# Reordering a fused two-attention and expert layer: projections moved into the first gap, transposed scores two slots sooner

## Time and profile before

| | |
|---|---|
| median of 3 runs | 625.67 us |
| profiled execution | 623.53 us |
| its span, first to last instruction | 621.8 us |
| PE busy | 521.4 us, 84% of the span |
| DVE, ACT, POOL busy | 55%, 35%, 24% |
| mean granted clock of PE | 0.946 |

### The profile page before, as it was taken

One profiled execution on the slowest core, in us unless ns is written; L12 is line 12 of the kernel. 1 busy time (PEld: TensorE's weight loads), 2 busy tenths in 40 slices (PEclk: granted clock), 3 DMA queues, 4 the chain that ended last, 5 costly groups with the idle time before them and its releaser, 6 DMA issues. The chain is left out here.

```text
span 621.8 us, 12823 instructions
## 1 busy us (share of the span) xinstructions
PE 521.4 (84%) x5092; PEld 404.6 (65%) x5092; DVE 339.1 (55%) x952; ACT 219.7 (35%) x491; POOL 147.3 (24%) x160
## 2 busy tenths in 40 slices
PE   6179395979799989989999789798798999999960
PEld 5047274756567767766767556577587888888850
DVE  2577265456667768768677957674263202232114
ACT  2014143335344544545554535353521111232103
POOL 4000011003004004004104166001124755132330
PEclk9599699889999999999999989799999999999995
DMA  5999907585785595685549556346666634897214
GB/s 163 118 132 139 161 10 127 68 108 69 94 127 82 89 144 70 100 135 69 91 77 136 85 104 191 66 148 190 229 229 228 204 51 74 247 304 241 23 20 138
DMA packets 58119, 78.96 MB, mean 127 GB/s; under 512 B 8734, under 2 KB 51357, under 8 KB 54988
## 3 DMA queue, kind: packets, MB, share of 16 engines
q1 hardware_dynamic: 41192, 39.34, 41.8%
q10 hardware_dynamic: 10724, 33.51, 16.4%
q0 software_dynamic: 6144, 5.29, 5.3%
HBM read 40.32 MB, written 13.74 MB: 87 GB/s over the span
## 5 line engine op out<-in xcount | busy, mean ns | idle before, releaser
L957 DVE TENSOR_REDUCE negm<-nat 128x4 f32<-128x512 f32 (+2 forms) x192 | 120.0, 641 | 84.3 <-PE nat L534 81.1
L769 ACT ACTIVATE probs<-byk 128x512 f32<-128x512 f32 (+1 forms) x192 | 105.6, 563 | 114.9 <-PE byk L534 100.4
L534 PE MATMUL nat<-arena 96*128 96x128 bf16 (+2 forms) x512 | 72.8, 245 | 0.0
L534 PE MATMUL byk<-arena 99*128 99x128 bf16 (+2 forms) x512 | 72.2, 244 | 0.0
L534 PEld LDWEIGHTS byk<-arena 99*128 99x128 bf16 x512 | 46.1, 100 | 17.9 <-issue 1.3
L534 PEld LDWEIGHTS nat<-arena 96*128 96x128 bf16 x512 | 46.6, 101 | 16.4 <-issue 2.5
L530 PE MATMUL nat<-window_q,identb 128*128 128x384 bf16 (+1 forms) x96 | 35.0, 365 | 18.8 <-DMA arena<-parts_k 12.7
L1213 POOL TENSOR_TENSOR resk<-fk,parts_k 128x512 f32<-128x512 f32 x8 | 9.3, 1159 | 158.0 <-ACT fk L710 107.2
L530 PE MATMUL byk<-window_k,identb 128*128 128x384 bf16 (+1 forms) x96 | 34.3, 357 | 13.4 <-DMA arena<-mT 12.7
L672 PE MATMUL work<-yn_T,arena 128*128 128x160 f32 x256 | 40.1, 305 | 2.4 <-DVE r_s L1124 2.4
L672 PE MATMUL work<-woT,arena 128*128 128x160 f32 x256 | 39.8, 304 | 0.0
(11 more groups left out here) (189 smaller groups left out, 912.6 us busy)
## 6 DMA issues: line engine op xcount, KB each, us to landing
arena<-parts_q SPq DMA_DIRECT2D x96, 128.0 KB, 5.1
arena<-parts_k SPq DMA_DIRECT2D x96, 128.0 KB, 5.2
arena<-in_ffn_wi ACTq DMA_DIRECT2D x12, 1024.0 KB, 5.2
arena<-in_ffn_wo ACTq DMA_DIRECT2D x12, 1024.0 KB, 8.3
expert_x<-ranked ACTq DMA_DIRECT2D x4, 650.0 KB, 5.2
v_s<-expert_x SPq DMA_DIRECT2D x20, 130.0 KB
xres<-in_x ACTq DMA_DIRECT2D x8, 256.0 KB, 5.9
token_y<-xres SPq DMA_DIRECT2D x8, 256.0 KB, 4.9
```

Of the source, the lines that this page charges most:

```text
L534: last = nc.tensor.matmul(bank[:, i * w:(i + 1) * w], lhsT, rhs, start=False, stop=(i == heads - 1), skip_group_check=True)
L769: nc.scalar.activation(dst, src, ACT.Exp, scale=0.25).then_inc(exp_ready, 1)
L957: V.tensor_reduce(dst, src, AX, ALU.max, negate=True).then_inc(nat_free[job % 2], 1)
```

## The change

It moves pieces of the plan and one of the loads; no computation is added or left out.

- Unit 2's QS, SQ and KS stand before the first N job, and its SK behind unit 0's first N job. Unit 3's four steps stand where unit 2's stood. `x3`, the input that unit 3's projection reads, is loaded at the start, and the clearing of `v_c` (`one_c`) goes to slot 13.5.
- `SOONER` is 2 for units 2 to 13: their T, PV, YA and YB stand two slots sooner (unit 2's already did).
- MT of units 3 to 13, and XL with it, stand 0.8 slots sooner (13.2 behind n0 and not 14).
- Y2, WO, R3 and L3 stand one slot later behind YB than before, so one slot sooner in all for units 3 to 11 and one later for units 0 to 2. The closing steps of units 4 to 13 that are c units stand two slots sooner, XR and RT about one.

```diff
--- before.py
+++ after.py
@@ -54,12 +54,14 @@
 X_SLOT = (0, 1, 2, 3, 0, 1, 2, 0)
 X_TURN = (1, 1, 1, 1, 2, 2, 2, 3)
 X_BEFORE = {4: 0, 5: 1, 6: 2, 7: 4}
-LOADS = ((-20, "x1"), (-19.9, "x2"), (-19.8, "wv"), (-19.7, "rows"), (-3, "one_s"), (-2, "one_c"), (11.52, "x3"), (11.58, "wo"),
+LOADS = ((-20, "x1"), (-19.9, "x2"), (-19.8, "wv"), (-19.75, "x3"), (-19.7, "rows"), (-1.2, "one_s"), (11.52, "wo"), (13.5, "one_c"),
          (24.7, "ck"), (24.75, "c0"), (24.8, "cq"), (38.3, "c1"), (38.4, "cv"), (50.1, "wr"))
 CLEARS = (4, 5, 6, 7)
 
 
-SOONER = {0: 5.1, 1: 3.4, 2: 2}
+SOONER = {0: 5.1, 1: 3.4}
+SOONER.update({k: 2 for k in range(2, 14)})
+AHEAD = {2: ((-25.5, "QS"), (-25.45, "SQ"), (-25.4, "KS"), (-23.4, "SK")), 3: ((-24.9, "QS"), (-24.45, "SQ"), (-24.4, "KS"), (-24.3, "SK"))}
 ROWS_BY_ACT = 12
 
 
@@ -104,10 +106,10 @@
                             add(n0 + (15.6 if b == 0 else 9.6), "LX", UNIT_OF["s", later])
             if b == 3:
                 add(n0 + 9.7, "LC", UNIT_OF["c", 2])
-            add(n0 + {0: 11.56, 1: 12.65, 2: 13.25}.get(b, 14.05), "XL", k)
-            for at, name in ((-12.9, "QS"), (-12.45, "SQ"), (-12.4, "KS"), (-12.3, "SK")) if b == 2 else ((-19, "QS"), (-18, "SQ"), (-17.5, "KS"), (-16.5, "SK")):
+            add(n0 + {0: 11.56, 1: 12.65}.get(b, 13.25), "XL", k)
+            for at, name in AHEAD.get(b, ((-19, "QS"), (-18, "SQ"), (-17.5, "KS"), (-16.5, "SK"))):
                 add(n0 + at, name, k)
-            for at, name in ((13.95 if b == 0 else 8.5, "VS"), (20, "XB"), (34 - sooner, "Y2"), (35 - sooner, "WO"), (36 - sooner, "R3"), (36.8 - sooner, "L3")):
+            for at, name in ((13.95 if b == 0 else 8.5, "VS"), (20, "XB"), (35 - sooner, "Y2"), (36 - sooner, "WO"), (37 - sooner, "R3"), (37.8 - sooner, "L3")):
                 add(n0 + at, name, k)
         else:
             if b + TOK < B:
@@ -115,14 +117,14 @@
             late = 2 if b == B - 1 else 0
             for at, name in ((-19, "KC"), (-18, "CK"), (late - 11.5, "XC"), (late - 10.2, "QC"), (late - 9.2, "SC"), (late - 6, "XA"), (10, "VC")):
                 add(n0 + at, name, k)
-            for at, name in CLOSING.get(k, ((n0 + 33.3, "FQ"), (n0 + 34.4, "R1"), (n0 + 35.2, "L1"), (n0 + 37, "R2"), (n0 + 37.7, "L2"),
-                                            (n0 + 39.4, "XS"), (n0 + 39.5, "XR"), (n0 + 40.9, "RT"))):
+            for at, name in CLOSING.get(k, ((n0 + 33.3 - sooner, "FQ"), (n0 + 34.4 - sooner, "R1"), (n0 + 35.2 - sooner, "L1"), (n0 + 37 - sooner, "R2"),
+                                            (n0 + 37.7 - sooner, "L2"), (n0 + 39.4 - sooner, "XS"), (n0 + 40.4 - sooner, "XR"), (n0 + 41.8 - sooner, "RT"))):
                 add(at, name, k)
         for j in range(JOBS):
             add(n0 + j, "N", k, j)
             add(t_slot(k, j), "T", k, j)
         add(n0 + (11.3 if k == 0 else 12), "MP", k)
-        add(n0 + {0: 11.5, 1: 12.6, 2: 13.2}.get(k, 14) if k < last else 195.6, "MT", k)
+        add(n0 + {0: 11.5, 1: 12.6, 14: 14}.get(k, 13.2) if k < last else 195.6, "MT", k)
         for g in range(G):
             add(n0 + 22.2 - sooner + 3 * g if k < last - 1 else t_slot(k, 3 * g + 2) + (1.1 if g < G - 1 else 0.5), "PV", k, g)
         add(n0 + 32.6 - sooner if k < last - 1 else (198.6, 206.9)[k - last + 1], "YA", k)
```

## The result

The changed kernel takes 636.84 us in the median of 4 runs (634.86 to 641.25), the kernel before beside it 624.78 (615.12 to 626.27, 4 runs): ratio 1.0264, 95% interval 1.0217 to 1.0311. It is **slower**; 618 us was forecast, with a range of 604 to 630.

A forecast was written before the change was run, and what follows sets the result against it. The prediction took PE, busy 521 of 622 us, as the bound, its waits moving the end. Terms 0.9 - 3.3 - 4.0 - 4.2 - 5.9 + 8.4 + 2.5 = -5.6 took 623.5 to 618 us, range 604 to 630.

The forecast's parts named there:

- (2): Unit 0's maxima rows stand behind unit 2's stacks in the DMA queue: first T at 55.5 us, 11.2 us later.
- (3): Unit 0's first T to unit 1's first T, at 77.6 us with a shorter wait; sum of the stacks part +0.9 us.
- (4): Unit 1's Y2: half of its 3.6 us wait and of the 2.9 us half clock behind it goes, -3.3 us.
- (5): Unit 3's Y2: YB comes two slots sooner, so its wait and half clock go, -4.0 us.
- (9): Unit 3's first T: longer wait for maxima rows behind unit 5's stacks, +1.3, and half clock, +1.2; together +2.5 us.
- (8): Less work between MT and first T: PE waits 2.3 us at units 5, 7, 9 and 1.5 at unit 4, +8.4 us.
- (6): Unit 11's Y2: YB comes before the routing work on DVE, so wait and half clock go, -4.2 us.
- (7): Other waits for YB (1.5), XR's (2.5) and N's behind MT at units 7 and 9 (1.9) go, together -5.9 us.
- C: Rival: maxima rows behind stacks at every unit, MT to T becomes the shortest way; about +29, 647 us; chance 0.10.
- D: Rival: no change, each wait that goes turns up at the next DVE result; 624 us; chance 0.12.
- A: Rival: maxima rows land in time, about 1.3 us from issue, so (8) falls away; 610 us; chance 0.15.
- B: Rival: DMA queues share, maxima rows served between SP's stacks, unit 0's first T at 45.6; 605 us; chance 0.13.

The follow-up runs named there:

- half early: The changed kernel with KS and SK of the third unit (unit 2) left where they were before; 638.63 us, ratio 1.0244 to the kernel before.
- T only: The kernel before with T, PV, YA and YB of units 3 to 13 two slots sooner, nothing else; 646.55 us against 621.15, 1.0391.
- one sooner: The kernel before with T, PV, YA, YB of units 3 to 13 one slot sooner, MT sooner at odd units 3 to 11, XR 0.7 later; 624.78 us, 1.0022.

## Why the prediction was wrong

**Right in the main, up to unit 5.** (2) Unit 0's first T at 55.5, measured 57.07; *half early* shows the queue to be the cause. (3) Unit 1's at 77.6, measured 78.00; this part +0.9 us, measured +1.5 (ratio 1.0024, which takes in 0). (4) Unit 1's Y2 -3.3: MT of unit 2 to MT of unit 3 shortened by 5.3 us. (5) -4.0: unit 4 to 5 shortened by 3.4. (9) Unit 3's T +2.5: unit 3 to 4, 26.63 us before and 29.13 after, +2.5. (8) At unit 4 1.5 us were forecast, and T waited 0.07. With that the terms up to MT of unit 5 are -2.4 in sum, measured -3.65: errors of up to 2 us in single terms, of either sign, offset each other, which is luck. (6) -4.2 is there in kind: unit 12 to 13 shortened by 2.8.

**The wait at T (8)** came out near its size at the odd units, 2.3 us each forecast at units 5, 7 and 9, 2.83, 1.93 and 1.27 measured, and the even units were covered. At units 7 and 9 that is luck: the rows need 2.7 to 2.9 us from their issue where 3.6 were taken, and the wait ends with ACT's exponential, held back by XL, which the prediction does not name.

**What failed** is the slot of MT. Step (8) counted the rows' way from MT and took mp to be there; step (7) even booked "L3 now ends before MP" as a gain of 1.9 us. The same sentence was the price: VectorE takes its steps in order, so what ends before MP delays MP. The wait of MT for mp stood at 0 in the sum and measured 11.1 us between units 5 and 15 (0.6 before), and putting L3 and L2 behind MP took 1.8 of the 2.6% away. The old kernel's rows had it. At the odd units MP ended some 0.8 us before MT began (226.37 and 227.17 at unit 7), and MT was to come 0.8 slot sooner with L3's 1.4 us put ahead. At the even units mp was only just in time, behind L1; I never asked where L1 and L2 stand. The second failure in (7) is N: I took N's waits behind L3 as gone, and they went, but four of 1.7 to 1.8 us for reductions are new at units 6, 8, 10 and 12, where L1 and L2 crowd VectorE. Of the -5.9 nothing is left in the sum: the waits of Y2 and XR that it counts did go, but in the table N's idle time grows by 2.8 us, and among the others 5.4 us of new ones (for ACT's yT and probs and for VectorE's res_sk) take their place. From MT of unit 5 to MT of unit 15 steps (6), (7) and (8) made some -3 us, and +17.9 were measured.

The prediction's reading of the clock, that a wait of over about 2 us brings the half clock, does not hold in the changed kernel: 2.83 us at unit 5 did not, and 1.74 us at unit 8 was followed by 0.52 (below).

**The rivals.** C named the right place, MT to T as the shortest way, and its cause, stacks in the queue, holds at units 3 and 5 (7.3 and 5.7 us from MT to T in the changed kernel) but not beyond: the even units do not wait at T at all there, and *T only*, which waits at every unit, does so behind unit 5 for a way of 3.8 to 5.2 us with few or no packets of stacks in flight, not of 7.2. D's sign, waits of N grown by as much as those of Y2 and XR shrank, was there (2.8 and 2.7 us), with the wait of MT on top. A (rows there about 1.3 us from their issue) and B (unit 0's first T at 45.6) are refuted by 2.7 to 2.9 us and by 57.07.

**Left open**: whether the 3.5 us of *one sooner* for ACT come from T, which gives ACT its work sooner; what brings the 3.9 us of PE's longer busy time; and how much time XL in its old slot, with all else as changed, would give back, since no run moves XL alone.

## What to carry to other kernels

When a step is moved sooner, follow the serial way that ends at it back over every engine (here reduction, MP, MT, maxima rows, T, and the exponential that empties T's bank) and ask at each link what now stands ahead of it on its engine; a wait that goes at one link comes back at the next. Freeing a consumer by moving it later, where its cover is, gained 0.4% in one run and 1% in another; moving what stands ahead of it sooner lost 2.6%. A step on an engine that works in order is never "out of the way" because it ends early: what stands behind it pays.

## What the runs showed of the hardware

The waits for mp at the even units differ, 2.04 us at units 6 and 10 but only 0.69 and 0.51 at units 8 and 12, although mp comes 3.2 to 3.3 us behind the last reduction at all four. PE's clock makes the difference. It runs the same pieces ahead of MT at full clock at unit 6 and at half clock at unit 8, behind 1.81 and 1.74 us of waiting at N, and so comes to MT later there:

```profile
199.10:200.90 1.80, 1.71 (x15) 1.25 (x15) 1.66 (x6) 1.32 (x4) 1.43 (x2) 1.00 0.30 81
249.80:252.90 3.10, 3.07 (x15) 2.10 (x15) 2.93 (x9) 1.72 (x4) 1.95 (x2) 0.52 0.25 73
```

At each of these units one step of VectorE takes some 1.1 us longer while GpSimd runs an operation of its own. At unit 6 it is xres, ahead of MP; at unit 8 GpSimd begins later, and it is a step of MP. VectorE at unit 6, then unit 8:

```profile
200.34 1.78 DVE L1037 TENSOR_SCALAR xres<-r_c,mv_c,rstd_c 128x256 f32<-128x256 f32 x2
202.25 0.19 DVE L968 TENSOR_TENSOR rm<-negm,mp 128x32 f32<-128x32 f32 x1
...
250.99 0.73 DVE L1037 TENSOR_SCALAR xres<-r_c,mv_c,rstd_c 128x256 f32<-128x256 f32 x2
251.84 1.28 DVE L968 TENSOR_TENSOR rm<-negm,mp 128x32 f32<-128x32 f32 x1
```

GpSimd at unit 6, then unit 8:

```profile
200.38 1.26 POOL L1230 TENSOR_TENSOR x<-x,rows 128x512 f32<-128x512 f32 x1 [0.37 <-PE work L476]
...
251.81 1.27 POOL L1230 TENSOR_TENSOR x<-x,rows 128x512 f32<-128x512 f32 x1 [1.15 <-PE work L476]
```

The Trainium skill says that an operation of VectorE and one of GpSimd can exclude each other from a shared port (SBUF — State Buffer, SBUF: two separate sides); these rows agree, though no run here moved GpSimd's operation to show it.
